# The last feed-forward of a four-layer kernel in four rounds of four batches

## The reference, cut to what matters

```python
# last layer: B = 16 batches, C = 128 channels, 256 tokens each
y = ctx @ Wo                      # ctx: attention, 16 heads of 8
r = y + q
h = layer_norm(r, ffn_ln_g, ffn_ln_b)          # over the 128 channels of a token
h = gelu(h @ W1 + b1) @ W2 + b2                # hidden width 256
out = transpose(h + r, (0, 2, 1))
```

## Time and profile before

| | |
|---|---|
| time, median of 3 runs | 2522.0 us (2519.47 to 2522.32) |
| profiled execution | time 2525.5 us, span 2523.8 us |
| mean granted TensorE clock | 0.942 |
| PE, DVE, ACT, POOL busy | 88%, 71%, 58%, 28% of the span |
| last attention's last `x` add (L2012) | starts at 2460.42 us |
| first and last stage of the feed-forward | copy at 2460.96 us, last `add` from 2520.35 us for 0.75 us |

### The profile page before, as it was taken

The page is one execution under the profiler, slowest core; times in us unless marked ns, Lnnn a source line. Parts: engine busy times, 40 slices in busy tenths (PEclk is TensorE's granted clock), DMA queues, the critical chain, the costliest instruction groups (busy, mean ns, idle before and its releaser), DMA issues. The chain is left out here.

```text
span 2523.8 us, 52976 instructions
## 1 busy us (share of the span) xinstructions
PE 2212.8 (88%) x17289; PEld 1776.9 (70%) x17289; DVE 1791.2 (71%) x4693; ACT 1468.7 (58%) x4021; POOL 709.0 (28%) x1041
## 2 busy tenths in 40 slices
PE   4999999995999999997988888699999696888886
PEld 3998989994998989987855555466666595555553
DVE  7666666667666666667578886888888663777756
ACT  2554545553555555555557676577777572777666
POOL 3011111111011111103034553566666204333200
PEclk7999999997999999998969998899999896899989
DMA  5100111000000000002000001000000000000000
GB/s 121 22 22 23 22 23 55 22 22 21 1 22 22 22 22 22 1 1 66 0 13 9 10 7 36 1 8 3 13 17 15 5 0 9 10 8 8 5 2 34
DMA packets 72947, 47.21 MB, mean 19 GB/s; under 512 B 29232, under 2 KB 71600, under 8 KB 72752
## 3 DMA queue, kind: packets, MB, share of 16 engines
q1 hardware_dynamic: 72752, 44.62, 6.7%
HBM read 41.45 MB, written 2.10 MB: 17 GB/s over the span
## 5 line engine op out<-in xcount | busy, mean ns | idle before, releaser
L1759 DVE TENSOR_REDUCE maxima<-bank 128x2 f32<-128x512 f32 x512 | 342.8, 684 | 108.3 <-PE bank L948 105.9
L1430 ACT ACTIVATE probs_t<-bank 128x512 f32<-128x512 f32 x512 | 282.7, 601 | 78.4 <-PE bank L939 75.7
L1306 ACT ACTIVATE wide_probs_t<-bank 128x256 f32<-128x256 f32 x256 | 98.5, 385 | 310.4 <-PE bank L828 308.2
L2085 POOL TENSOR_TENSOR wide_columns<-wide_pair_columns,zero 128x8 f32<-128x8 f32 x16 | 3.2, 202 | 863.4 <-DVE x L1656 821.8
L1311 ACT ACTIVATE wide_probs<-bank,wide_neg_max 128x129 f32<-128x129 f32 x512 | 184.1, 365 | 84.7 <-DVE wide_neg_max L1626 80.1
L1318 ACT ACTIVATE wide_heads_high<-bank,wide_columns 128x128 fp32r<-128x128 f32 x512 | 160.3, 365 | 96.2 <-PE bank L840 94.8
L1631 DVE RECIPROCAL wide_inverse<-wide_sums 128x2 f32<-128x2 f32 x256 | 42.5, 166 | 224.4 <-ACT wide_probs L1311 224.4
L1645 DVE SCALAR_TENSOR_TENSOR wide_heads_low<-bank,wide_columns,wide_heads_high 128x128 fp32r<-128x128 f32 x512 | 155.3, 345 | 41.2 <-ACT wide_heads_high L1318 35.8
L939 PE MATMUL bank<-q_packed,k_packed 32*128 32x256 f32 x1024 | 175.0, 341 | 8.7 <-ACT probs_t L1430 8.5
L1466 ACT ACTIVATE probs<-scores_masked,neg_max 128x128 f32<-128x128 f32 x512 | 163.3, 394 | 24.1 <-DVE neg_max L1942 22.5
L948 PE MATMUL bank<-k_packed,q_packed 32*128 32x256 f32 x1024 | 172.2, 346 | 4.8 <-ACT q_packed L1415 2.2
(11 more groups left out here) (296 smaller groups left out, 6878.9 us busy)
## 6 DMA issues: line engine op xcount, KB each, us to landing
cn<-in_ctx SPq DMA_DIRECT2D x48, 128.0 KB, 2.0
wide_pair_weights<-in_L_xattn_wq SPq DMA_DIRECT2D x16, 256.0 KB, 2.8
wide_pair_weights<-in_L_xattn_wk SPq DMA_DIRECT2D x16, 256.0 KB, 3.2
wide_pair_weights<-in_L_xattn_wv SPq DMA_DIRECT2D x16, 256.0 KB, 3.7
wide_pair_weights<-in_L_xattn_wo SPq DMA_DIRECT2D x16, 256.0 KB, 3.4
q_packed<-max_rows SPq DMA_DIRECT2D x256, 4.0 KB
wide_ctx_rows<-in_ctx SPq DMA_DIRECT2D x4, 512.0 KB, 4.2
x<-in_x SPq DMA_DIRECT2D x4, 512.0 KB, 5.3
```

What stands on the lines that cost most here:

```text
L1430: act.activation(probs_t[j % 8][:, :], shifted_bank[j % 2][:, :], ACT.Exp, bias=0.0).then_inc(s.exp_ready, 1)
L1759: dve.tensor_reduce(maxima[pack // 2][:, b, pack % 2, :], head_scores[packed_scores(1 - u, j)][:, :].rearrange("p (a k) -> p a k", a=UNITS ...
```

## The change

The feed-forward goes in four rounds of four batches (`TURNS3 = 4`), each in two halves `h` of two batches. A round has one chain of statistics and roots over eight tiles (two banks) in place of two chains over four. PE transposes straight from `x`, so the ACT copy and `rows3` are gone. The rounds are written out, with no loop, so `x` is indexed by constants. `hidden3_in`, `hidden3` and `result` exist twice, `norm3` has eight tiles. The halves use banks 0 and 1 (turned), 2 and 3 (turned back), 4 and 5, 6 and 7 (up products; the down product goes back into 4 or 6).

Round 0 moves in part into the attention's written-out windows: `turn3(0)` behind step `TURN3 = 5` of window 31 on PE, `moments3(0)` and both `normalize3(0, h)` behind step `NORM3 = 11` of window 31 on DVE, and `back3(0, 0)` behind step `BACK3 = 14` of window 32 on PE. Batches 0 to 3 are final in `x` by then. The core of the diff:

```diff
@@ PE @@
+                    if conclude and not following and (core or carry):
+                        conclude(core, j)
...
+        def turn3(r):
+            pe.wait_ge(packed.x_added, B + 4 * (r + 1))
+            if r == 0:
+                pe.wait_ge(packed.max_ready, HN * 2 * B)
+            for h in range(SLOTS):
+                for u in range(SLOTS):
+                    for n in range(2):
+                        last = pe.transpose(bank[h][:, (2 * u + n) * P:(2 * u + n + 1) * P], x[:, 4 * r + 2 * h + u, n * P:(n + 1) * P],
+                                            ident[:, :])
+                last.then_inc(ff3.turned, 1)
+        def back3(r, h):
+            s = ff3
+            pe.wait_ge(s.rows_normed, SLOTS * r + h + 1)
+            if r == 0:
+                pe.wait_ge(packed.exp_ready, HN * 2 * B)
+            else:
+                pe.wait_ge(s.in_ready, SLOTS * (r - 1) + h + 1)
+            for m in range(4):
+                last = pe.transpose(bank[2 + h][:, m * P:(m + 1) * P], norm3[:, 4 * h + m, :], ident[:, :])
+            last.then_inc(s.turned_back, 1)
...
+            def conclude(core, j):
+                if core and j == TURN3:
+                    turn3(0)
+                if not core and j == BACK3:
+                    back3(0, 0)
...
-            def turn(i):
-                pe.wait_ge(s.x_copied, i + 1)
...
+            def up(r, h):
+                i = SLOTS * r + h
                 pe.wait_ge(s.in_ready, i + 1)
+                if r:
+                    pe.wait_ge(result_ready, i - 1)
+                elif h == 0:
+                    pe.wait_ge(packed.heads_copied, B)
+                else:
+                    pe.wait_ge(packed.x_added, 2 * B)
                 for f in range(2):
-                    pe.matmul(bank[2 + f][:, :], w3_up[:, f * P:(f + 1) * P], hidden3_in[:, :], start=True, stop=True)\
+                    pe.matmul(bank[4 + 2 * h + f][:, :], w3_up[:, f * P:(f + 1) * P], hidden3_in[h][:, :], start=True, stop=True)\
                       .then_inc(s.up_ready, 1)
+            def down(r, h):
+                i = SLOTS * r + h
                 for f in range(2):
                     pe.wait_ge(s.hidden_ready, 2 * i + f + 1)
-                    if f == 0:
-                        after(pe, result_ready, i)
-                    last = pe.matmul(bank[4][:, :], w3_down[:, f, :], hidden3[:, f, :], start=f == 0, stop=f == 1)
+                    last = pe.matmul(bank[4 + 2 * h][:, :], w3_down[:, f, :], hidden3[h][:, f, :], start=f == 0, stop=f == 1)
                 last.then_inc(s.down_ready, 1)
...
+            back3(0, 1)
+            for r in range(TURNS3):
+                more = r + 1 < TURNS3
+                if more:
+                    turn3(r + 1)
+                for h in range(SLOTS):
+                    up(r, h)
+                for h in range(SLOTS):
+                    down(r, h)
+                if more:
+                    for h in range(SLOTS):
+                        back3(r + 1, h)
@@ ACT @@
-            def copy(i):
-                after(act, s.turned, i)
-                act.sem_inc(idle, 1)
-                act.activation(rows3[:, :, :], x[:, ds(SLOTS * i, SLOTS), :], ACT.Copy).then_inc(s.x_copied, 1)
...
+            for r in range(TURNS3):
+                for h in range(SLOTS):
+                    i = SLOTS * r + h
+                    act.wait_ge(s.turned_back, i + 1)
+                    after(act, s.up_ready, 2 * (i - 1))
+                    act.activation(hidden3_in[h][:, :], bank[2 + h][:, :], ACT.Identity, bias=ln3[:, 5:6], scale=ln3[:, 4:5])\
+                       .then_inc(s.in_ready, 1)
+                for h in range(SLOTS):
+                    i = SLOTS * r + h
+                    after(act, s.down_ready, i - 1)
+                    for f in range(2):
+                        act.wait_ge(s.up_ready, 2 * i + f + 1)
+                        act.activation(hidden3[h][:, f, :], bank[4 + 2 * h + f][:, :], ACT.Gelu, bias=b3_up[:, f:f + 1])\
+                           .then_inc(s.hidden_ready, 1)
@@ DVE @@
+            def conclude(j):
+                if j == NORM3:
+                    moments3(0)
+                    for h in range(SLOTS):
+                        normalize3(0, h)
...
+        def moments3(r):
+            dve.wait_ge(ff3.turned, SLOTS * (r + 1))
+            after(dve, ff3.rows_normed, SLOTS * r)
+            chain = Chain(dve, ff.chain, 2 * ROUNDS * (NORM_TWO + 1) + (statistics_steps(8) + 6) * r)
+            row_statistics(dve, chain, [bank[h][:, m * P:(m + 1) * P] for h in range(SLOTS) for m in range(4)], stats3, idle)
+        def normalize3(r, h):
...
+            after(dve, ff3.turned_back, SLOTS * (r - 1) + h + 1)
+            for m in range(4):
+                c = 4 * h + m
+                ins = dve.tensor_scalar(norm3[:, c, :], bank[h][:, m * P:(m + 1) * P], stats3.mean_var[:, c, 0:1], stats3.rstd[:, c:c + 1],
+                                        ALU.subtract, ALU.mult)
...
+            ins.then_inc(ff3.rows_normed, 1)
+            chain.join()
...
+            for r in range(TURNS3):
+                more = r + 1 < TURNS3
+                if more:
+                    moments3(r + 1)
+                for h in range(SLOTS):
+                    if more:
+                        normalize3(r + 1, h)
+                    add(r, h)
```

More of the change, by code:

```diff
@@ L103, in __init__ @@
     def __init__(self, sem):
-        self.x_copied = sem("ff3_x_copied")
+        self.stored = [sem(f"ff3_stored{h}") for h in range(SLOTS)]
         self.turned = sem("ff3_turned")
@@ L903, in feed_forward, with attention @@
             products(first + ROUNDS - 1, False)
[L905 removed]
+        def attention(third, w_q, source_q, w_k, w_v, when, conclude=None):
             s = packed
@@ L1206, in layer3 @@
             pe.wait_ge(packed_ready, 3)
-            attention(1, w_queries[:, :], lambda b: x[:, ds(b, 1), :].rearrange("p a d -> p (a d)"), w3[:, 1, :], w3[:, 2, :], SCHEDULE3)
+            attention(1, w_queries[:, :], lambda b: x[:, ds(b, 1), :].rearrange("p a d -> p (a d)"), w3[:, 1, :], w3[:, 2, :], SCHEDULE3,
+                      conclude)
         def feed_forward3():
             s = ff3
-            def turn(i):
-                pe.wait_ge(s.x_copied, i + 1)
-                for u in range(SLOTS):
-                    for n in range(2):
-                        last = pe.transpose(bank[0][:, (2 * u + n) * P:(2 * u + n + 1) * P], rows3[:, u, n * P:(n + 1) * P], ident[:, :])
-                last.then_inc(s.turned, 1)
@@ L1219, in products @@
-            def products(i, more):
-                pe.wait_ge(s.rows_normed, i + 1)
-                for u in range(SLOTS):
-                    for n in range(2):
-                        last = pe.transpose(bank[1][:, (2 * u + n) * P:(2 * u + n + 1) * P], norm3[:, u, n * P:(n + 1) * P], ident[:, :])
-                last.then_inc(s.turned_back, 1)
-                if more:
-                    turn(i + 1)
-                pe.wait_ge(s.in_ready, i + 1)
+            def up(r, h):
+                i = SLOTS * r + h
+                pe.wait_ge(s.in_ready, i + 1)
+                if r:
[4 more added lines that the diff above has]
+                    pe.wait_ge(packed.x_added, 2 * B)
@@ L2042, in feed_forward3 @@
         def feed_forward3():
             s = ff3
-            steps = statistics_steps(4) + 3
-            def norm(i):
-                chain = Chain(dve, ff.chain, 2 * ROUNDS * (NORM_TWO + 1) + steps * i)
-                dve.wait_ge(s.turned, i + 1)
-                after(dve, s.turned_back, i)
-                dve.sem_inc(idle, 1)
-                norm_columns(chain, [bank[0][:, k * P:(k + 1) * P] for k in range(4)],
-                             [norm3[:, k // 2, k % 2 * P:(k % 2 + 1) * P] for k in range(4)], s.rows_normed)
-                dve.wait_ge(s.rows_normed, i + 1)
-                assert chain.steps == steps, (chain.steps, steps)
@@ L2420, in _ @@
         attend(1, 5, packed.placed, 2)
-        with sp.Fori(0, ROUNDS) as i:
+        for i in range(ROUNDS):
             sp.wait_ge(result_ready, i + 1)
-            sp.dma_start(out[ds(SLOTS * i, SLOTS)].rearrange("b p d -> p b d"), result[:, :, :]).then_inc(out_stored, 16)
-        sp.wait_ge(out_stored, 16 * (ROUNDS + 1))
+            sp.dma_start(out[SLOTS * i:SLOTS * (i + 1)].rearrange("b p d -> p b d"), result[i % SLOTS][:, :, :])\
+              .then_inc(ff3.stored[i % SLOTS], 16)
+        for h in range(SLOTS):
+            sp.wait_ge(ff3.stored[h], 16 * ROUNDS // SLOTS)
 def position_code():
```

72 lines of the change are left out of this document (25 added, 47 removed).

## The result

The changed kernel takes 2486.19 us (median of 4, 2483.9 to 2487.97), the kernel before took 2520.73 us (median of 4, 2514.4 to 2522.32; three of the four are the runs known ahead of the prediction, the fourth took 2514.4): a ratio of 0.9878 [0.9851, 0.9904], 34.5 us less. The forecast was 2501.2 us and the range ended at 2496.5: the sign was right, the gain larger. Both intervals hold ratios near 0.990, some 25 us.

What follows compares the result with a forecast made beforehand. DVE was taken as the bound. Feed-forward rounds of 10.3 us plus first and last round moved the end from 2521.1 to 2499.9, gaining 21.2, less 0.4 in the tail: 2522.0 - 20.8 = 2501.2 us, range 2496.5 to 2507.0.

Steps and rivals of the forecast that it cites:

- The steady round: Feed-forward: a round of four batches takes 10.3 us where two old rounds take 12.8.
- Moments: Steady round on DVE: statistics, means and one root chain for eight columns take 4.8 us.
- Turnaround: Steady round: DVE waits for PE's transposes back and turned before the next statistics, 1.9 us.
- The last round: Feed-forward's end: statistics at 2482.6, half 1 normalised at 2491.0, last add done at 2499.9.
- The first statistics: Feed-forward's start: round 1's statistics begin at 2462.0, under 1.5 us behind the last x add.
- The tail: Attention's end: round 0's eight transposes between steps 5 and 6 of window 31 cost 0.4 us; DVE's block fits.
- the cover of 7.90 us: DVE's idle time before batch 14's x add in the tail, said to hold round 0's moments and normalisings, 0.3 us spare.
- I forecast 2522.0 - 20.8: Whole kernel: the old median less the forecast gain gives 2501.2 us.
- Medians may lie some 1.5 us off: Whole kernel: allowance for measurement spread in the range, as three times of the kernel before span 2.9 us.
- The tail gains too: Rival, chance 0.14: eight transposes keep the clock up in the attention's tail; 2499.2 us, 2498 at best.
- PE becomes the bound: Rival, chance 0.12: feed-forward records cost 0.6 us each, sixteen take 9.6 not 7.4; 4.5 us more, 2505.7.
- The low clock holds: Rival, chance 0.04: half clock through the feed-forward makes rounds 17.5 us; 2529 us, slower than before.

Runs made afterwards that it cites:

- e1: Kernel before plus eight unread 128x128 transposes of x behind step 5 of window 31; 0.9997 of the kernel before's time.
- c4: Kernel before, unchanged, fourth profile, one execution: tail 19.8 us at clock 1.00, feed-forward 58.7 us.
- the second comparison: Changed kernel, unchanged, timed again against more runs of the kernel before: 2495.24 against 2517.34 us, ratio 0.9901.
- c8: Second profile of e1's kernel, one execution: tail 23.6 us at clock 0.78, feed-forward 58.8 us.
- c9: Third profile of e1's kernel, one execution: tail 23.6 us at clock 0.78, feed-forward 58.8 us.
- e8: Kernel before with unread transposes in the feed-forward's PE waits (40, 8 and 6); 0.9998 of the kernel before's time.
- c7: Second profile of e8's kernel, one execution: tail 25.8 us at clock 0.67, feed-forward 57.5 us at 1.00.
- e3: Kernel before with the feed-forward's four hardware loops written out, copies kept; 1.0000 of the kernel before's time.
- c10: Fourth profile of e1's kernel, one execution: tail 19.8 us at clock 1.00, feed-forward 60.5 us.
- e4: Changed kernel with one chain of statistics and roots per half in place of one for both; 0.9960 of the kernel before's time.
- e6: e4 with 12 and 8 unread 128x128 transposes filling PE's waits each round; 0.9949 of the kernel before's time.
- e7: e4 with three and two unread 128x256 products filling PE's waits; 0.9947 of the kernel before's time.

## Why the prediction was wrong

**The steady round: right mechanism, too long by 0.7.** The forecast had 10.3 us, the trace shows 9.63. Moments: 4.8 forecast, 2451.62 - 2446.91 = 4.71. From there to the end of the second normalising: 3.64 forecast, 2453.56 + 1.36 - 2451.62 = 3.30, since operations on DVE that stand in one run start some 0.1 us before the one ahead has ended (2451.62 + 1.36 = 2452.98, and the `add` starts at 2452.90), and the sum added full durations. Turnaround: 1.9 forecast, 2456.54 - 2454.92 = 1.62. I had taken the old gap of 1.39 us and put four more transposes of 0.12 on it; twelve in one run take 2455.47 + 1.04 - 2454.97 = 1.54 us, and only 0.08 lies around them.

**The last round.** Forecast 8.4 + 0.55 + 7.55 + 0.8 = 17.3, measured 2482.55 - 2466.17 = 16.38. The products took 2481.80 - 2474.73 = 7.07 us, 7.55 forecast: in an unbroken run a record comes 0.43 us behind the one before (8 take 3.60 with a last one of 0.6), where I had 0.46 from a row of four. The other 0.4 is that of moments and normalisings, as in the steady round.

**The first statistics** stood 2446.91 - 2445.54 = 1.37 us behind the last `x` add, 1.6 forecast. From that add to the end of the last `add` the sum gave 2499.9 - 2460.4 = 39.5 us; the trace has 2482.55 - 2445.54 = 37.0. The missing 2.5 are 0.2 + 2 times 0.7 + 0.9. So the step that failed in the sum is the pricing of runs on DVE and PE by whole durations from short rows. It made three terms too long, all in one direction: the way through the normalisings (3.64 for 3.30), the turnaround (1.9 for 1.62) and the last products (7.55 for 7.07). By itself that is 2.5 of 21.2 us.

**The tail.** The sum took 0.4 us for the turns, nothing for the block on DVE, and left the low clock in place. At full clock the move costs 0.4 us (20.2 against 19.8), and that the number came out is luck. The turns cost nothing: e1, which has them alone, takes 19.8 us. The block of statistics and normalisings costs all of it. Behind it the `x` add of batch 14 starts with no idle time, in the changed kernel 16.7 us behind the last maxima:

```profile
2439.54 2.64 DVE L2085 TENSOR_SCALAR norm<-bank,mean_var,rstd 128x128 f32<-128x128 f32 x8
2442.10 0.41 DVE L2038 TENSOR_TENSOR x<-x,bank 128x256 f32<-128x256 f32 x1
```

In c4, the kernel before at full clock, it starts 14.7 us behind them:

```profile
2444.93 0.42 DVE L2012 TENSOR_TENSOR x<-x,bank 128x256 f32<-128x256 f32 x1 [5.22 <-PE bank L1086]
```

So the cover of 7.90 us was read at half clock. At full clock it is 5.22 us, the block of 2442.18 - 2434.90 = 7.3 us (7.6 forecast) does not fit, and the add is 2.0 us late, of which 0.4 reach the last `x` add.

**The frame.** The larger part of the miss is not in the sum: "I forecast 2522.0 - 20.8" takes all of the program ahead of window 31 and the clock of the tail as fixed. This is the step that put the time outside the range. The one takes 2425.3 to 2434.6 us in four profiles of before (2425.4 to 2431.2 in three of after), the other 19.8 or some 25.8 us, and the profile of before had the long end of both. The sentence "Medians may lie some 1.5 us off" was the second step that failed: medians of the kernel before lay at 2514.4, 2517.1, 2517.3 and 2520.7 us in four comparisons, those of the changed kernel at 2486.2 and 2495.2. A feed-forward of 22.4 to 23.7 us less and a tail between 0.4 us more and 6.0 us less give the 22.1 us of the second comparison and most of the 34.5 of the first; the rest is spread ahead of window 31, and no run says what causes it. Against its own baseline the second gain is 1.3 us above the 20.8 forecast, but 2495.24 us too lies below the range.

**The rivals.** "The tail gains too" came true in the profiles, but with the wrong cause, for the turns do not hold the clock (c8, c9), and at too low a price. It had the 14.5 us from step 6 to the `x` add of batch 14 shrink by 3; at full clock they are 2444.93 - 2435.49 = 9.4 us (c4). Its 2 us net were 5.4 to 6.0 (20.2 against 25.6 to 26.2). The rule of the Trainium skill that spoke against it did not decide it: the clock answers to transposes here (e8, c7), and the tail falls with them all the same (c8, c9). "PE becomes the bound" did not happen: PE finished both down products at 2450.09 + 3.60 = 2453.69, S + 6.8 with S = 2446.91, ahead of the second `add` at 2454.84. "The low clock holds" did not either: 1.00 in each stretch. The table loads were off the path (e3 for the loop; the single load of 1.28 us at 2446.78 lies under PE's products). That the copies of the steady round were off it too was not run by itself.

## What to carry to other kernels

When short dependent steps of fixed cost are on the path, put more columns into each: 0.17 us on four or eight made 2.55 us a round. Price an unbroken run by the distance between starts in a long row, not by the whole duration of a short one. And before a gain of one per cent is forecast against a median, profile the kernel before more than once: a stage that comes out at two lengths is not a baseline.

## What the runs showed of the hardware

- TensorE's granted clock is not a function of the instructions alone. The same tail ran at 1.00 (2.4 GHz) in 4 of 9 profiles and fell to 0.50 (1.2 GHz) in 5, in steps 4 to 6 of window 31 each time, where PE has a wait of 0.68 us that the full ones have as well (c4), and stayed there for some 17 us although PE was then busy 5.00 of 5 us. With eight transposes put in behind step 5 it fell in 2 of 4 (e1, c8, c9, c10) and stayed for 10 us. Why it falls in one execution and not in the next is open.
- With dead transposes of 128x128 in the waits the clock of a stretch was 1.00 in place of 0.66 (e4 to e6, one profile each), dead products did the same (e7), and the feed-forward was 2.9 and 3.3 us shorter. In the kernel before they raised the clock of the feed-forward from 0.89 to 0.91 (ten profiles) to 0.97 and 1.00 (e8, c7), which gave some 1.4 us, and the times (0.9998) can't tell that from nothing.
- On ScalarE a table load took 1283 ns on both lines and in e3, and the loop of the kernel before repeated it twice a turn: written out, one of fourteen was left (e3).
- A step of the root on DVE took 0.17 us on four columns and on eight, and the next, which needs its result, started 0.20 us behind its start (2449.41 and 2449.61).
